# Two heads' queries and keys stacked by transfers instead of matmuls, joint score products, and the experts' rows mixed on TensorE

## The reference, cut to what matters

```
q = (x @ Wq.T + bq)   k = (x @ Wk.T + bk)   v = (x @ Wv.T + bv)      # 32 heads of 16 features
scores = einsum('bhqd,bhkd->bhqk', q, k) / sqrt(16)
scores = where(causal, scores, -inf);  att = softmax(scores)
out = einsum('bhqk,bhkd->bhqd', att, v) ... @ Wo.T + bo

logits = x @ gate_w;  topv, topi = top_k(logits, 2);  w = softmax(topv)
out = sum over the 2 chosen experts of  w_e * (x @ expert_w[e])
```

## Time and profile before

| what | value |
|---|---|
| median of 3 runs | 1710.32 us (1709.1 to 1710.33) |
| the profiled execution's own time | 1712.04 us |
| its span | 1710.3 us |
| mean granted TensorE clock | 0.962 of full |
| busy PE, DVE, ACT, POOL | 91%, 71%, 48%, 55% |

### The profile page before, as it was taken

How to read it: one execution, slowest core, us unless ns; L and a number is a source line. 1 busy time by engine, 2 the same in 40 slices (tenths; PEclk the granted TensorE clock), 3 DMA queues, 4 the chain that set the end, 5 groups by cost and what they waited for, 6 DMA issues and landing times.

```text
span 1710.3 us, 26565 instructions
## 1 busy us (share of the span) xinstructions
PE 1549.1 (91%) x8870; PEld 1215.7 (71%) x8870; DVE 1222.2 (71%) x2024; ACT 826.1 (48%) x1639; POOL 945.8 (55%) x861
## 2 busy tenths in 40 slices
PE   5899999999999999999999879996899999987791
PEld 3677877878778778778787657874567767666681
DVE  5778788778778787877887866567466677767525
ACT  3464554554555545455554423331276666663231
POOL 4367576676675766776756851007442344327544
PEclk9999999999999999999999889998899999997796
DMA  3111012021110110211101111221000000032435
GB/s 119 38 50 59 17 50 64 12 79 38 48 61 18 49 61 12 80 37 49 61 19 50 56 56 62 74 99 37 1 14 1 14 1 1 28 146 75 133 133 166
DMA packets 49498, 92.61 MB, mean 54 GB/s; under 512 B 8016, under 2 KB 32720, under 8 KB 44176
## 3 DMA queue, kind: packets, MB, share of 16 engines
q1 hardware_dynamic: 45744, 79.58, 14.4%
q0 software_dynamic: 3680, 12.06, 2.1%
HBM read 81.14 MB, written 10.49 MB: 54 GB/s over the span
## 4 chain that ended last, share of the span: by engine, by line
PE 59%; DVE 17%; POOL 8%; issue 7%; ACT 6%; DMA 3%; SPq 0%; POOLq 0%; DVEq 0%; ACTq 0%
PE banks L360 28%; PE banks L1666 6%; DVE tap L1237 4%; PE banks L1943 3%; PE banks L1803 3%; PE banks L1731 2%; PE banks L1908 2%; PE banks L1725 2%; PE banks L1696 2%; DMA x<-in_w_gate 2%; PE banks L1933 2%; POOL wol L365 2%; PE banks L1740 2%; DVE xbc L1243 1%; DVE acc L629 1%
## 5 line engine op out<-in xcount | busy, mean ns | idle before, releaser
L1237 DVE SCALAR_TENSOR_TENSOR tap<-banks,parg,tap 128x511 f32<-128x511 f32 (+2 forms) x288 | 215.0, 747 | 26.9 <-ACT tap L943 19.6
L723 POOL TENSOR_TENSOR am<-ah,upto 128x1024 fp32r<-128x1024 f32 x64 | 121.6, 1901 | 179.7 <-PE banks L1696 138.6
L874 POOL TENSOR_SCALAR kz<-kst,head 128x512 fp32r<-128x512 f32 x64 | 99.0, 1564 | 160.3 <-DVE kst L1493 160.3
L360 PE MATMUL banks<-xTh,wch 128*128 128x512 f32 x384 | 162.8, 424 | 5.2 <-DVE em L1343 3.7
L951 ACT ACTIVATE th<-tap 128x512 f32<-128x512 f32 x96 | 60.7, 632 | 215.0 <-DVE tap L1237 212.9
L360 PE MATMUL banks<-xTh,wcl 128*128 128x512 f32 x384 | 151.2, 394 | 0.0
L360 PE MATMUL banks<-xTl,wch 128*128 128x512 f32 x384 | 150.7, 393 | 0.0
L1169 ACT ACTIVATE prob<-banks,nmax 128x128 f32<-128x128 f32 (+3 forms) x256 | 121.6, 529 | 55.3 <-DVE nmax L1504 55.1
L1504 DVE TENSOR_REDUCE nmax<-banks 128x2 f32<-128x256 f32 (+3 forms) x128 | 104.7, 818 | 40.5 <-PE banks L1934 40.3
L723 POOL TENSOR_TENSOR am<-al,upto 128x1024 fp32r<-128x1024 f32 x64 | 122.1, 1908 | 0.0
L1343 DVE TENSOR_TENSOR em<-banks,gmask 128x1024 f32<-128x1024 f32 x64 | 78.2, 1221 | 49.8 <-ACT banks L992 48.9
(11 more groups left out here) (290 smaller groups left out, 4393.1 us busy)
## 6 DMA issues: line engine op xcount, KB each, us to landing
x<-grownT SPq DMA_DIRECT2D x96, 128.0 KB, 4.8
x<-in_w_conv SPq DMA_DIRECT2D x7, 1536.0 KB, 6.5
x<-in_w_gate SPq DMA_DIRECT2D x8, 1024.0 KB, 4.9
x<-in_w_out SPq DMA_DIRECT2D x8, 1024.0 KB, 4.8
eraw<-in_expert_w SPq DMA_DIRECT2D x8, 1024.0 KB, 7.3
gur<-in_ff_gu SPq DMA_DIRECT2D x7, 1024.0 KB, 4.7
x<-in_hidden SPq DMA_DIRECT2D x16, 256.0 KB, 3.6
mates<-yd SPq DMA_DIRECT2D x8, 512.0 KB, 4.6
```

The lines of the kernel that those rows point to most:

```text
L360: m = nc.tensor.matmul(o, a, b, start=first and n == 0, stop=last and n == len(terms) - 1)
L723: m = pool.tensor_tensor(am[:, part, :, :], a[:, i, :].bitcast(F32).unsqueeze(2).to_broadcast([P, HG, P]), upto[:, :].unsqueeze(1).to_broa ...
L874: m = pool.tensor_scalar(kz[:, quad % 2, p2, j, :], kst[:, p2, :].bitcast(F32), head[:, j:j + 1], None, ALU.mult)
L1237: nc.vector.scalar_tensor_tensor(tap[:, q % 2, sh:L], bk(CONV_BANKS[q % 2])[:, 0:L - sh], parg[:, KC * q + k:KC * q + k + 1], tap[:, q % 2 ...
```

## The change

1. The selection matmuls, `kst`, `selz`, `head` and the POOL copies go. The stacks are written by transfers from SBUF to SBUF that SP issues: for a quad 6 of 32 x 512 (`qs`) and 12 of 16 x 512 (`kz`), 18 together, 288 in all. The zeros of `kz` and of the unused rows of `qs` are written once by POOL. A quad's transfers count on the semaphore `qk_in` of its parity; PE waits for it before a quad's first unit, and ACT before it overwrites `qh` (`high`).
2. The projections stand in four pieces of 3 matmuls, at s = 3 to 6 and 8 to 11. ACT multiplies the query weights and bias by 1/sqrt(16).
3. For qi = 0 and 1 both heads' scores are one product into one bank, and so is the mask. Before, a head's product had at least 256 columns.
4. At the end DVE writes diagonal matrices `share` (identity times weight), PE makes each token tile's mix as two fp32 products into the tile's own bank, and DVE reads that bank in the norm. ACT has no part in it. SP keeps up to four loads of `mates` under way.

```
-            for at, what in ((0, ("k", 0, 1)), (1, ("k", 1, 1)), (2, ("q", 0, 1)), (3, ("q", 1, 1))):
-                if s == at:
-                    return (m,) + what
-            for at, what in ((5, ("proj", 0, 0)), (6, ("proj", 0, 1)), (8, ("proj", 1, 0)), (9, ("proj", 1, 1)),
-                             (11, ("k", 0, 0)), (12, ("k", 1, 0)), (13, ("q", 0, 0)), (14, ("q", 1, 0))):
-                if s == at and m + 1 < AT * NB:
-                    return (m + 1,) + what
+            for w, at in ((0, (3, 4, 5, 6)), (1, (8, 9, 10, 11))):
+                if s in at and m + 1 < AT * NB:
+                    return m + 1, w, at.index(s)
...
+        STACK = 2 * (3 + 3 * 2)
+        def stacked(quad):
+            return 16 * STACK * (quad // 2 + 1)
...
@@ block.sync
+                for m in range(AT * NB):
+                    for u in range(2):
+                        quad = 2 * m + u
+                        if quad >= 2:
+                            sp.wait_ge(s_ready, 8 * (quad - 1))
+                        for w in range(2):
+                            sp.wait_ge(qk_l, 2 * m + w + 1)
+                            for p2 in range(2):
+                                of = 32 * (2 * u + p2)
+                                for r, part in enumerate((qh, ql, qh) if w == 0 else (qh, qh, ql)):
+                                    if w == 0:
+                                        sp.dma_start(qs[32 * r:32 * r + 32, quad % 2, p2, :].bitcast(F32), part[of:of + 32, w, :].bitcast(F32)
+                                                     ).then_inc(qk_in[quad % 2], 16)
+                                    else:
+                                        for j in range(2):
+                                            row, at = of + HD * j, 32 * r + HD * j
+                                            sp.dma_start(kz[at:at + HD, quad % 2, p2, j, :].bitcast(F32), part[row:row + HD, w, :].bitcast(F32)
+                                                         ).then_inc(qk_in[quad % 2], 16)
+                    t = m // NB
+                    if m % NB == 0 and t + 1 < AT:
+                        sp.wait_ge(aq_lo, 2 * t + 2)
+                        sp.dma_start(aqr[:, 0, :, :], wq[t + 1]).then_inc(aq_in, 16)
+                        sp.dma_start(aqr[:, 1, :, :], wk[t + 1]).then_inc(aq_in, 16)
...
@@ block.scalar, high(m, w)
                     act.wait_ge(qk_ps, 2 * m + w + 1)
+                    if m:
+                        for u in range(2):
+                            act.wait_ge(qk_in[u], stacked(2 * (m - 1) + u))
...
@@ block.tensor, unit n
                         if n % 8 == 0:
-                            pe.wait_ge(kpad, 2 * quad + 2)
-                            pe.wait_ge(st_q, 2 * quad + 2)
+                            pe.wait_ge(qk_in[quad % 2], stacked(quad))
                         if n >= 2:
                             pe.wait_ge(exp_ready, n - 1)
-                        for j in range(2):
-                            o = bk(2 * (n % 2) + j)
-                            kn = max(kw, 2 * P)
-                            mat(o[:, 0:kn], qs[:, quad % 2, p2, qi * P:kw], kz[:, quad % 2, p2, j, 0:kn], start=True, stop=False)
-                            m = mat(o[:, kw - P:kw], identb[:, :], future[:, :], start=False, stop=True)
+                        for heads in ((0, 2),) if qi < 2 else ((0, 1), (1, 2)):
+                            o, many = scores(n)[:, heads[0]:heads[1], :], heads[1] - heads[0]
+                            mat(o, qs[:, quad % 2, p2, qi * P:kw], kz[:, quad % 2, p2, heads[0]:heads[1], 0:kw], start=True, stop=False)
+                            m = mat(o[:, :, kw - P:kw], identb[:, :], future[:, :].unsqueeze(1).to_broadcast([P, many, P]),
+                                    start=False, stop=True)
...
@@ block.tensor, the end
+                pe.wait_ge(yb_out, SLOT_TILES)
+                for i in range(NT):
+                    pe.wait_ge(share_ready, TOP * (i + 1))
+                    mates_there(pe, i)
+                    for c in range(TOP):
+                        m = mat(bk(i), share[:, i, c, :], mates[:, i, c, :], start=(c == 0), stop=(c == TOP - 1))
+                    m.then_inc(mixed, 1)
...
@@ block.vector, the end
+                dve.wait_ge(yx_ps, SLOT_TILES)
                 for i in range(NT):
-                    dve.wait_ge(scaled, i + 1)
-                    nc.vector.scalar_tensor_tensor(acc[:, i, :], mates[:, i, 1, :], rt[:, 3, i:i + 1], acc[:, i, :],
-                                                   ALU.mult, ALU.add).then_inc(mixed, 1)
+                    for c in range(TOP):
+                        nc.vector.tensor_scalar(share[:, i, c, :], ident[:, :], rt[:, 2 + c, i:i + 1], None,
+                                                ALU.mult).then_inc(share_ready, 1)
+                for i in range(NT):
                     norm_round(4, i)
```

More of the change, by code:

```diff
@@ L230, in program @@
         mates = sd("mates", [P, NT, TOP, DM])
+        share = sd("share", [P, NT, TOP, P])
         D.close()
@@ L306, in program @@
         yd_out = [sem(f"yd_out{n}") for n in range(2)]
-        back_in = [sem(f"back_in{n}") for n in range(2)]
-        scaled, mixed = sem("scaled"), sem("mixed")
+        share_ready, mixed = sem("share_ready"), sem("mixed")
         stored = sem("stored")
@@ L428, in unit, with scores @@
             return n // 8, n % 8 // 2, n % 2
+        def scores(n):
+            qi = unit(n)[1]
+            kw = (qi + 1) * P
+            if qi < 2:
+                return bk(2 * (n % 2))[:, 0:2 * kw].rearrange("p (j k) -> p j k", j=2)
+            return banks[:, 2 * (n % 2):2 * (n % 2) + 2, 0:kw]
         def heads_of(quad):
@@ L580, in _ @@
                 sp.wait_ge(v_f, NT)
-                sp.wait_ge(st_ps, 4 * QUADS)
+                for n in range(2):
+                    sp.wait_ge(qk_in[n], stacked(QUADS - 2 + n))
                 for e in EARLY:
@@ L866, in _ @@
                     low(pool, awl[:, k, :], awr[:, k, :], awh[:, k, :]).then_inc(aw_lo, 1)
-                def padded(quad, p2):
-                    pool.wait_ge(st_k, 2 * quad + p2 + 1)
-                    if quad >= 2:
-                        pool.wait_ge(s_ready, 8 * (quad - 1))
-                    for j in range(2):
-                        m = pool.tensor_scalar(kz[:, quad % 2, p2, j, :], kst[:, p2, :].bitcast(F32), head[:, j:j + 1],
-                                               None, ALU.mult)
-                    m.then_inc(kpad, 1)
-                for p2 in range(2):
-                    padded(0, p2)
                 for n in range(UNITS):
-                    piece = pieces(n)
-                    if piece and piece[1] == "k":
-                        padded(2 * piece[0] + piece[3], piece[2])
                     if n % 32 == 14 and n // 32 + 1 < AT:
@@ L1168, in _ @@
                                 act.wait_ge(pt_ps, 2 * w + 1 + j)
[L1169 removed]
+                            e = nc.scalar.activation(prob[:, n % 2, j, 0:kw], scores(n)[:, j, :], ACT.Exp,
                                                      bias=nmax[:, n % 2, j:j + 1])
@@ L1173, in _ @@
                         if piece:
-                            m, what, i, u = piece
-                            if what == "proj" and u == 1:
-                                high(m, i)
-                            if what == "q":
-                                queries(2 * m + u, i)
+                            m, w, part = piece
+                            if part == KT - 1:
+                                high(m, w)
                         if n % 32 == 14 and n // 32 + 1 < AT:
@@ L1211, in _ @@
                         nc.scalar.copy(yb[:, i % 4, :], bk(2 + i % 2)).then_inc(yb_out, 1)
-                act.wait_ge(r_dve, 4)
-                for i in range(NT):
-                    act.wait_ge(back_in[i % 2], 16 * (i // 2 + 1))
-                    nc.scalar.activation(acc[:, i, :], mates[:, i, 0, :], ACT.Copy, scale=rt[:, 2, i:i + 1]).then_inc(scaled, 1)
         @block.vector
@@ L1535, in _ @@
                     if piece:
-                        m, what, i, u = piece
-                        if what == "proj" and u == 1:
-                            lows(m, i)
-                        if what == "k":
-                            keys(2 * m + u, i)
+                        m, w, part = piece
+                        if part == KT - 1:
+                            lows(m, w)
                 dve.wait_ge(wide_in, 32)
@@ L1914, in _ @@
                 for w in range(2):
-                    for part in range(2):
+                    for part in range(KT):
                         project(0, w, part)
-                for what, i in ORDER:
-                    stack(0, what, i, 0)
                 pe.wait_ge(v_f, NT)
-                pe.wait_ge(sel_ready, SEL + 2)
+                pe.wait_ge(sel_ready, SEL + 3)
                 for n in range(UNITS + O_BACK - 7):
@@ L1957, in _ @@
                     if piece:
```

(2 more changed lines are left out.)

100 lines of the change are left out of this document (27 added, 73 removed).

## The result

| | before | after |
|---|---|---|
| median, in the same comparison | 1708.62 us (1706.29 to 1710.33, 18 runs) | 1711.99 us (1707.37 to 1718.66, 18 runs) |
| profiled execution, span | 1712.04, 1710.3 us | 1710.41, 1708.7 us |
| seven rounds, first scores to the last round's | 249.66 us | 257.81 us |
| last round, to its last score product | 27.89 us | 27.01 us |
| first issue of `mates` to the end | 33.2 us | 28.3 us |

What follows compares the result with a forecast made beforehand. PE was taken to set the loop's pace and DVE the end's. Seven rounds 15.4 us, last round 2.8, end 1.4, clock -4.8 made 14.8 us less: 1695.5 us, range 1688 to 1703, 8 in 10 from 1673 to 1713.

Steps and rivals of the forecast that it cites:

- Parts 1 and 2: In the loop: removing the stacks saves 3.7 us a round (4.4 of PE), joint scores 0.9 (1.1 of PE).
- a microsecond taken off PE in the loop is thus worth 0.85: Loop's factor from comparing ten units of rounds 6 and 7: 8.0 us of PE's time cost 6.85 us.
- The 31.2: Forecast length in us of a loop round without further waits: 35.8 - 3.7 - 0.9.
- I give them nothing: The projections' smaller pieces in the loop are the same matmuls in smaller portions, so priced at 0 us.
- Part 3: Key transfers before each round: 12 issues of 0.47 us, 9.1 us in all against PE's 6.7; PE stops 2.4 us.
- Part 4: Half clock for 3.5 us behind a round-start stop loses about 1.6 us; charged in 3 of 7 rounds, 4.8 us.
- all rounds at half clock: Rival: all seven round starts run at half clock after the stop, 6.4 us more, 1702 us; chance 0.10.
- Part 5: Loop's start and last round: the start changes by 0, the last round gets 2.8 us shorter.
- Part 6: Kernel's end: PE's mixing products set the turn, 1.9 us a tile at full clock, `share` hidden; 1.4 us gained.
- Slower: SP's queue: Rival: an issue on SP costs 0.74 us, PE stands 6.4 us, rounds are 37.6, time 1730 us; chance 0.22.
- transfers hidden: Rival: the loop's transfers cause no stop, 36.4 us less, 1674 us; chance 0.16.

Runs made afterwards that it cites:

- before_defer: The kernel before with only DVE's low part written one unit later in DVE's order; 1709.54 us, ratio 1.0005.
- half_stacks: The kernel before without the second matmul (the low part's) of each stack, so scores differ; 1704.17 us, ratio 0.9969.
- kf_two: keys_first with each projection in two pieces of 6 matmuls, at s = 5, 6 and 8, 9; 1684.56 us, ratio 0.9853.
- kf_defer: keys_first with all pieces one unit earlier and DVE's low part one unit later in DVE's order; 1674.05 us, ratio 0.9791.
- keys_first: The changed kernel with the key projection ahead of the query projection, leaving 6 transfers instead of 12 behind the last piece; 1689.36 us, ratio 0.9884.
- fewer: The changed kernel with 6 key transfers of 32 rows a quad in place of 12 of 16, so scores differ; 1685.69 us, one run.
- price_list: The changed kernel with seven batches of six transfers behind the last store; an issue took 0.61 to 0.63 us SBUF to SBUF, 0.44 to 0.45 otherwise.
- kf_lowlate: keys_first with DVE's low part alone one unit later, pieces in their old places; 1682.32 us, ratio 0.9835.

## Why the prediction was wrong

The mechanism was named and is there: a stop of PE at each round's start, released by the keys' transfers, and the clock at half behind it. What turned the sign is a size, that of the round without any stop, and the first two points below make it up.

1. **Parts 1 and 2, "a microsecond taken off PE in the loop is thus worth 0.85".** This is the step that failed most. It priced the stacks from a comparison of a round with preparation and one without, in which mostly projection pieces stood; and in the round without, DVE's and ACT's share of the preparation was gone too. Taking away only PE's share leaves the other engines' share in place. Which of their waits took up the rest isn't shown; DVE's stand for ACT alone was not it, by before_defer. half_stacks measured 0.4 in place of 0.85. Joint scores gave 0.4 a round for 0.9. Stacks and joint scores gave 2.9 (35.9 to kf_two's 33.0) for 4.6. The 31.2 was within reach: kf_defer, with other places for the pieces and the low part, has 31.4.
2. **"I give them nothing"**, the four pieces: 0.9 us a round (keys_first against kf_two). With the first point the round without a stop is 33.9 in place of 31.2: 2.7 x 7 = 19 us.
3. **Part 3, the price of an issue**: 0.63 us, not 0.47. The stop became 3.4, not 2.4. Yet it cost less than its length: behind it the transposes found all copies done. In round 6 of after, where the clock did not fall at the start, the first two units took 1.14 and 1.44 us, in keys_first 2.20 and 1.39 in even rounds and 3.05 to 3.11 and 1.39 in odd ones, that is 1.0 and 1.9 more; the other units but the last are alike. The last, with the stop of 3.0 in it, took 3.2 us more than keys_first's. Net 2.2 against its even rounds and 1.4 against its odd ones, 1.8 on average; with the mean stop of 3.4 it is 2.2, a little under the 2.4 that were forecast.
4. **Part 4, the clock**: half clock for 3.4 us (once 6.8) at six of seven round starts; 3 of 7 were charged. The first two or three units behind a stop took 1.1 to 1.3 us more in rounds 2 to 5 than in round 6, so a fall costs about 1.3, where 1.6 was forecast. The rival "all rounds at half clock" was nearer than the 3 of 7. The Trainium skill's page "TensorE: Matmul & The Clock Gate" (HAM oscillation) says that a loop which waits for a transfer each pass starts each pass at half rate; the trace agrees in six of seven.
5. **Part 5**: the loop's start took 15.1 instead of 14.2 us from the first high part to the first score, where 0 was booked. Again it is the 12 issues: with six (fewer) it took 11.3. The last round gained 0.9, not 2.8.
6. **Part 6, the end**: 4.9 gained, 1.4 forecast. From the first use of `mates` to the eighth moments it is now 15.5 us (1684.21 to 1699.69), where 18.4 was forecast. The clock rose 2.8 us after PE's first product, not 6.1, which is luck in part: in four of the other traces it rose 5.5 to 5.9 after it, which cost 1.5 us; a record costs 0.43 us at full clock (a turn of four 1.72), not 0.48; and behind the last moments POOL's power and DVE's normalizing are 0.8 us cheaper together. That the end's turn is PE's product and that `share` is hidden was right.

The seven rounds: forecast 10.6 us less with the clock, measured 8.2 more, a miss of 18.8. The last round and the start add 1.9 and 0.9, the end takes back 3.5.

The queue did not turn the sign, though an issue came out beyond the 0.59 us that the rival "Slower: SP's queue" named. That sum has a slip: 7 x 3.8 + 11.2 is 37.8, and the stop that balances 36.4 is 3.6 us, an issue of 0.57. A stop of 3.4 with all rounds at half clock gives 7 x 3.4 + 11.2 = 35.0 there, still 1.4 us faster than before, and the stops cost less than their length. In the prediction's own sum it takes the 2.7 us a round of the first two points to make the kernel slower. Against the round as it was, 33.9, the stops did decide: without them the kernel is 1.2% faster (keys_first). The rival "transfers hidden" is that kernel, and its 1674 missed by 15 us, for the most part by the same 2.7 a round.

Of the Trainium skill's rule on small transfers ("DMA: Bandwidth & Descriptors", Rules for kernel authors), which wants small transfers joined, the trace bears out the direction and not the price: the fixed 2 us of its Anatomy section, which describes transfers issued by GpSimd, is near the landing's 2.0 for SyncE's here and was paid once a stop, while the 12 issues of 0.63 us were paid in full.

Open stays why the clock spared the start of round 6: the stop before round 7 was as long, 3.00 us, and the clock fell behind it. Open stays too why it fell once in keys_first and fewer without a long stop, and how much of kf_defer's 2.5 us is the order in DVE and how much the place of the pieces.

## What to carry to other kernels

Work taken off the busiest engine is worth what the next engine's order leaves of it: price a removal with the removed work alone taken out, not with a stretch in which the other engines' share is gone as well. Where work moves to a DMA queue, count the issues that stand behind the last producer and let the producer with most transfers come first; here that alone was worth 22.6 us and turned a kernel slightly slower than before into a faster one. A stop of the matmul engine can also cost the clock behind it, here about 1.3 us in six of seven rounds, so a stop of 3 us a round is the first thing to remove.

## What the hardware showed that was not expected

- An issue on SyncE's queue costs 0.61 to 0.63 us when both ends are in SBUF, from 16 to 128 rows of 2 KB, and 0.44 to 0.47 for plain rows when one end is in HBM (price_list and the earlier trace rows); the broadcast loads of `grownT` from HBM took 0.70.
- Six of the seven stops of TensorE in after, 3.0 to 3.9 us long, came with a granted clock of 0.50 to 0.51 for 3.4 us (once 6.8). In five it fell within 0.8 us after TensorE was at work again, in the first of them during the stop; of two stops of 3.00 us one was followed by it and one not. Shorter stops of 1.77 and 2.26 us were followed by it in kf_lowlate, those of 1.07 to 1.29 were not. The loop is 84% busy all the same.
- The changed kernel's runs spread over 11.3 us, those of before over 4.0. The slower ones have the lower mean clock: the four slowest of 18, 1716.7 to 1718.7 us, stand at 0.952 to 0.954, the four fastest, 1707.4 to 1709.6, at 0.958 to 0.960. So the spread fits a varying number of such falls; only the profiled run shows them one by one.
- DVE's normalizing of 128 x 512 took 0.80 to 0.81 us from PSUM in after. From SBUF, in before, it took 1.27 or more for seven tiles while POOL was at work in SBUF, but 0.53 for the first tile (1684.80), when POOL stood idle: the company made it dear, and PSUM by itself is not the faster source. POOL's power of 128 x 1 took 0.98 to 1.00 us for the first seven tiles of before and 0.55 for the eighth; in after it took 0.55 to 0.57 for all.
